# Projection pieces moved from the middle of each quarter to its end, in the attention stage of a two-layer kernel

## The chip, the cores and the metric

The kernel runs on one core of a Trainium2 chip. The metric is the device time of one execution in microseconds (us), as the median of several runs. TensorE (PE) does the matmuls, VectorE (DVE), ScalarE (ACT) and GpSimd (POOL) the rest; the sync engine's queue (SP) issues the transfers.

## The reference

Two layers on x of 8 sequences of 512 rows with 256 columns. What matters here is the attention in both, 16 heads of 16 dimensions each:

```python
def _L0_attn_ref(x, Wq, bq, Wk, bk, Wv, bv, Wo, bo, head_mask):   # layer one
    q = (x @ Wq.T + bq).reshape(b, s, HEADS, HEAD_DIM)            # k, v alike
    attn = jax.nn.softmax(jnp.einsum('bqhd,bkhd->bhqk', q, k) / 4, axis=-1)
    out = jnp.einsum('bhqk,bkhd->bqhd', attn * head_mask, v).reshape(b, s, HIDDEN)
    return out @ Wo.T + bo
def _attention(x, wq, wk, wv, wo):                                # layer two
    q = q * cos + _rotate_half(q) * sin                           # k alike
    scores = jnp.where(causal, -jnp.inf, jnp.einsum('bhqd,bhkd->bhqk', q, k) * scale)
    out = jnp.einsum('bhqk,bhkd->bhqd', jax.nn.softmax(scores, axis=-1), v)
    return out @ wo
x = _layernorm(x + attention_one(x))
h = x + _attention(_rmsnorm(x, g1), ...)
x = _layernorm(x + h + moe(_rmsnorm(h, g2)))
```

(shortened: the last line stands for the residual, the mixture of 8 experts with the two best taken per row, and the final norm.)

## The kernel before

One program runs through setup, attention of both layers, router, experts and final norm. The change is in `attention_layers` alone.

There are 16 **units** `u`: units 0 to 7 are the sequences in layer one (`plain`, unmasked), 8 to 15 the same in layer two (`causal`, masked). A unit has four **groups** `n = 4u + g` of four heads, a group four **quarters**. Every engine runs `for n in range(FIRST, LAST): for quarter in range(4)` with n from -10 to 74, so that work of several units goes on at once. In one quarter of group n TensorE does:

- **scores** of group n (`score`, L772): q and k of 49 rows, that is half the height of the array (rows 0 or 64 up), 512 columns or fewer into one of three banks `ps_s`. ScalarE takes the exponential of each into `probs` (L969), and a score waits until the exponential of the score three before is done (`free_score`).
- **maxima** for group n + 3 (`maximum`, `causal_maximum`, L777): the same product turned, at the other half of the height, into one of three banks `ps_m`; VectorE reduces each to its row maxima (L1038), and `free_maximum` is the wait alike. The row maxima shift the scores three groups later.
- the **product with v** (`weigh`, L865): `probs` times v into `ps_o`, full height, four tiles of 32 columns, 512 moving columns unmasked, in a masked unit 512, 384, 256 and 128 for the tiles 0 to 3 of k. Quarters 2 and 3 do tiles 0 and 1 of group n, quarters 0 and 1 tiles 2 and 3 of group n - 1. ScalarE moves `ps_o` out in quarter 2 (`empty_o`, L976).
- one **piece** (`a_piece`): a part of other units' work, all into the one bank `ps_x`, by the table `piece_at(n, i)`. Long pieces are `qk` (six matmuls of 512 columns, L660), `v` (L671) and `out` (L704), twelve of 256 columns; short ones are `rows` (four transposes of the maxima, L692), and in masked units `turn` (x, L681), `parts` (L713) and `logits` (L723). A piece waits until the piece before it has been moved out of `ps_x` (`piece_out`), by ScalarE (L896, L899, L907, L915, L920, L926) or VectorE (L1099, L1106, L1112, L1123, L1128), each in its `empty_piece`.

An unmasked quarter has 4 scores and 4 maxima of 512 columns. In a masked unit `score_items` lists 4, 4, 2 and 2 scores, one in each quarter being a **diagonal** bank of four blocks of 128 columns, and a quarter has 3 maxima, one of them diagonal too. `diagonals` does both: a matmul of the mask into either bank (L834, L839), then eight blocks of 128 columns that add to it, scores and maxima in turn.

Before, the order within a quarter is pairs 0 and 1, piece, diagonals, pairs 2 and 3, product with v. ScalarE empties the piece of a quarter in the same quarter: behind its last exponential in unmasked units, behind the second or the first in masked ones (`early`); VectorE in the same way behind the first or the last reduction.

Besides, ScalarE does `whiten` and `part_high` in groups g = 1 and 2 and `square` in g = 3; VectorE does `part_low` and `statistics` in g = 3, `scale_hidden` in g = 1, in masked units the two halves of the rotation (`rope_cos` in even groups, `rope_sum` in odd ones), and `invert` in quarter 1 of odd groups. GpSimd splits q and k into a high and a low half (L529, L534), normalises the result (`normalise`, L542 to L548), splits weights for later (L605, L607) and, masked, computes `part_low` (L598).

The sync queue is in order too. In even groups it issues `swap` (q32 to q_swap, L362), which waits until the last qk piece of a half is emptied, then `load_qk` (six loads into qkx, L382, which wait for the store of the same half), then x or the residual's rows, the store of o, weights, and `load_o`; in odd groups `load_rows`, stores of the inverse and of o, `load_inv`, weights and `store_qk` (L367). TensorE waits for qkx at the first maximum of each even `ahead = n + 3`, so in odd groups n. The table of pieces is

```python
(0, 0): ("turn", u + 2, 0), (0, 1): ("turn", u + 2, 1), (0, 2): ("v", u + 1, 0), (0, 3): ("v", u + 1, 1),
(1, 0): ("parts", u - 3, 1), (1, 1): ("rows", u, 1), (1, 2): ("qk", u + 2, 0), (1, 3): ("qk", u + 2, 1),
(2, 0): ("logits", u - 3, 0), (2, 2): ("out", u - 1, 0), (2, 3): ("out", u - 1, 1),
(3, 0): ("parts", u - 2, 0), (3, 1): ("rows", u + 1, 0), (3, 2): ("qk", u + 2, 2), (3, 3): ("qk", u + 2, 3)
```

Of the kernel before, what the change touches and what calls it, by code (L numbers as in the profile page):

```python
# [22 lines left out]
G, HG = 4, 4  # L23
# [185 lines left out]
def attention_layers(nc, t, xT_dram, x_dram, x1_dram, matrices):  # L209
# [16 lines left out]
    causal = lambda u: B <= u < NU  # L226
# [8 lines left out]
    def piece_at(n, i):  # L235
# [4 lines left out]
            (1, 0): ("parts", u - 3, 1), (1, 1): ("rows", u, 1), (1, 2): ("qk", u + 2, 0), (1, 3): ("qk", u + 2, 1),  # L240
            (2, 0): ("logits", u - 3, 0), (2, 2): ("out", u - 1, 0), (2, 3): ("out", u - 1, 1),
            (3, 0): ("parts", u - 2, 0), (3, 1): ("rows", u + 1, 0), (3, 2): ("qk", u + 2, 2),
# [14 lines left out]
    def emptied_piece(engine, *piece):  # L257

        engine.wait_ge(piece_out, numbers[piece] + 1)

# [4 lines left out]
    with ExitStack() as ctx:  # L265
# [373 lines left out]
        def _(pe):  # L639
# [168 lines left out]
            def causal_maximum(n, quarter, i):  # L808
# [6 lines left out]
                if i == 0:  # L815
# [7 lines left out]
            def diagonals(n, ahead, quarter):  # L823
# [4 lines left out]
                if score_here:  # L828
                    i = 2 if quarter < 2 else 1
                    kind, o, k = score_items(n // G, quarter)[i]  # L830
                    number = items(n) + scores_before(n // G, quarter) + i
# [3 lines left out]
                if maximum_here:  # L835
                    number = items(ahead) + 3 * quarter + 1
# [32 lines left out]
            for n in range(FIRST, LAST):  # L869
                for quarter in range(4):  # L870
                    for i in range(2):
                        score(n, quarter, i)
                        maximum(n + 3, quarter, i)
                        if i == 0:
# [12 lines left out]

        @block.scalar
        def _(act):
# [124 lines left out]
            for n in range(FIRST, LAST):  # L1014
                u, g = n // G, n % G
                for quarter in range(4):
                    early = (1 if quarter < 2 else 0) if causal(u) else 3
                    for i in range(4):
# [4 lines left out]
                        if i == early:  # L1023
                            empty_piece(n, quarter)
# [10 lines left out]
        def _(vector):  # L1035
# [17 lines left out]
            def causal_row_max(n, quarter, i):  # L1053
# [5 lines left out]
                if i == 0:  # L1059
# [3 lines left out]
                elif i == 1:  # L1063
# [96 lines left out]
            def empty_piece(n, quarter):  # L1160
# [686 lines left out]
```

## Time and profile before

| | |
|---|---|
| median of 3 runs | 1531.02 us (1530.84 to 1533.89) |
| profiled execution | 1533.58 us, its span 1531.9 us |
| TensorE matmuls busy | 1288.0 us, 84% of the span |
| VectorE, ScalarE, GpSimd busy | 969.1, 830.7, 685.3 us |
| mean granted TensorE clock | 0.932 of full speed |
| attention stage | to about 890 us from the start of the span |

Times in the rows are us from the start of the span unless marked ns. A row of the timeline has the start, the duration, the engine, the line of the kernel, and in brackets how long the engine was idle before and what ended that; rows of one line close together are merged, with their count behind the x. A matmul's duration includes its way through the array, so the distance between starts tells what it occupies.

### The profile page before, as it was taken

How to read it: one execution, taken by the hardware profiler on the slowest of the kernel's cores; microseconds unless marked ns; L12 is line 12 of the kernel's file. 1: busy time of each engine (PE TensorE's matmuls, PEld its weight loads, DVE VectorE, ACT ScalarE, POOL GpSimd, SP SyncE). 2: the span in 40 equal slices, each digit the busy share in tenths (PEclk: the TensorE clock that was granted, in tenths of full speed). 3: DMA queues.
4: the chain of work that ended last, by engine and by line, in shares of the span. 5: the costliest groups of instructions: out<-in, count | busy, mean ns of one | idle time of the engine just before them, and what ended most of it. 6: DMA issues, size and time to landing. Idle time of an engine off the chain costs nothing. (4 is left out here: it accounts for less than half of the span.)

```text
span 1531.9 us, 32817 instructions
## 1 busy us (share of the span) xinstructions
PE 1288.0 (84%) x11210; PEld 715.7 (47%) x11278; DVE 969.1 (63%) x1778; ACT 830.7 (54%) x1669; POOL 685.3 (45%) x713
## 2 busy tenths in 40 slices
PE   1899999999999999999999831499999999999910
PEld 0222232323233444444444310388888888888810
DVE  6478888988897788787777317343444434444346
ACT  3158788888878676666666620133443334433313
POOL 1324365546455756666564442423343343433312
PEclk9979999999999999999999965599999999999965
DMA  4426566766676878778665438191111111111136
GB/s 122 83 56 168 158 164 180 194 164 177 190 208 172 207 210 213 200 193 213 205 177 164 144 126 244 52 329 55 45 47 42 41 44 45 47 42 41 39 120 220
DMA packets 162441, 212.20 MB, mean 139 GB/s; under 512 B 28577, under 2 KB 124321, under 8 KB 162337
## 3 DMA queue, kind: packets, MB, share of 16 engines
q1 hardware_dynamic: 154848, 190.38, 45.4%
q0 software_dynamic: 7488, 20.46, 4.5%
q8 instruction: 62, 1.02, 0.3%
q14 instruction: 43, 0.34, 0.1%
HBM read 119.55 MB, written 82.58 MB: 132 GB/s over the span
## 5 line engine op out<-in xcount | busy, mean ns | idle before, releaser
L969 ACT ACTIVATE a_probs<-a_ps_s 128x512 f32<-128x512 f32 (+2 forms) x896 | 460.6, 570 | 175.6 <-PE a_ps_s L772 172.8
L1038 DVE TENSOR_REDUCE a_shift_max<-a_ps_m 128x1 f16<-128x512 f32 x512 | 320.6, 683 | 68.9 <-PE a_ps_m L777 67.5
L1555 PE MATMUL e_ps_gu<-e_xT,w_up 128*128 128x256 f16 x2574 | 298.9, 274 | 2.2 <-ACT e_xT L1610 2.1
L777 PE MATMUL a_ps_m<-a_qkx 48*128 48x128 f16 (+3 forms) x1408 | 284.0, 301 | 13.7 <-DVE a_shift_max L1038 7.7
L772 PE MATMUL a_ps_s<-a_qkx 49*128 49x128 f16 (+3 forms) x1408 | 275.6, 296 | 15.9 <-ACT a_probs L969 14.8
L1555 PEld LDWEIGHTS e_ps_gu<-e_xT,w_up 128*128 x2574 | 249.8, 98 | 36.4 <-issue 7.1
L865 PE MATMUL a_ps_o<-a_probs,a_v_one 128*32 128x512 f32 (+3 forms) x2048 | 235.5, 533 | 2.6 <-ACT a_o L976 2.5
L772 PEld LDWEIGHTS a_ps_s<-a_qkx 49*128 49x128 f16 x1408 | 90.4, 95 | 290.9 <-ACT a_probs L969 154.1
L1517 POOL DMA_INDIRECT y<-e_y,e_put x78 | 76.9, 986 | 263.3 <-DVE e_y L1644 251.4
L1577 PE MATMUL e_ps_y<-w_down,e_h 128*128 x1404 | 162.6, 273 | 8.0 <-issue 6.1
L1655 DVE TENSOR_TENSOR e_h<-e_gate,e_ps_gu 128x512 f32<-128x512 f32 (+2 forms) x156 | 82.7, 551 | 127.9 <-ACT e_gate L1618 114.3
L1618 ACT ACTIVATE e_gate<-e_ps_gu 128x512 f32<-128x512 f32 x78 | 46.6, 597 | 203.9 <-PE e_ps_gu L1555 193.9
L1577 PEld LDWEIGHTS e_ps_y<-w_down,e_h 128*128 128x128 f16 x1404 | 127.9, 97 | 40.4 <-issue 14.6
L542 POOL TENSOR_TENSOR a_o_half<-a_o_half,a_inv_half 128x512 f32<-128x512 f32 x32 | 40.7, 1271 | 236.9 <-DMA a_inv_half<-a_inv_dram 236.9
L1661 DVE TENSOR_TENSOR e_h<-e_h 128x512 f16<-128x512 f32 (+2 forms) x156 | 83.3, 555 | 98.0 <-ACT e_h L1622 43.2
L1038 DVE TENSOR_REDUCE a_neg_off<-a_ps_m 128x1 f32<-128x384 f32 (+2 forms) x256 | 138.4, 544 | 9.6 <-PE a_ps_m L777 8.7
L1038 DVE TENSOR_REDUCE a_neg_max<-a_ps_m 128x4 f32<-128x512 f32 x128 | 88.0, 687 | 51.4 <-PE a_ps_m L777 48.6
L660 PE MATMUL a_ps_x<-a_xT,w_proj 128*128 128x512 f16 x384 | 102.9, 408 | 18.6 <-POOL a_xT L510 16.1
L777 PEld LDWEIGHTS a_ps_m<-a_qkx 48*128 48x128 f16 x1408 | 84.3, 94 | 54.6 <-DVE a_shift_max L1038 36.2
L529 POOL CAST a_qk<-a_q 128x1024 f16<-128x1024 f32 x32 | 33.2, 1037 | 163.5 <-DVE a_q L1093 101.3
L1504 POOL DMA_INDIRECT e_x<-part,e_take x78 | 83.3, 1068 | 43.5 <-issue 43.2
L704 PE MATMUL a_ps_x<-w_proj,a_aT 128*128 128x256 f16 x384 | 53.2, 294 | 32.5 <-POOL a_aT L548 24.0
(191 smaller groups left out, 1583.0 us busy)
## 6 DMA issues: line engine op xcount, KB each, us to landing
a_qkx<-a_qk_dram SPq DMA_DIRECT2D x192, 128.0 KB, 4.4
a_qk_dram<-a_qk SPq DMA_DIRECT2D x32, 512.0 KB, 5.6
a_o_dram<-a_o SPq DMA_DIRECT2D x64, 256.0 KB, 3.7
a_o_half<-a_o_dram SPq DMA_DIRECT2D x32, 256.0 KB
a_inv_half<-a_inv_dram SPq DMA_DIRECT2D x32, 256.0 KB
part<-a_part SPq DMA_DIRECT2D x16, 512.0 KB, 5.8
a_q_swap<-a_q SPq DMA_DIRECT2D x64, 128.0 KB
c_rows<-y SPq DMA_DIRECT2D x16, 512.0 KB, 5.5
```

The source lines that it names most:

```text
L660: mm = pe.matmul(ps_x[:], t.w_proj[:, 4 * layer + w, wh, k, m * P:(m + 1) * P], xT[:, u % 2, xh, k, :], start=n == 0, stop=n == 5)
L772: return pe.matmul(out, kx[first:first + 49, r, pair, kt * P:(kt + 1) * P], qx[first:first + 49, r, pair, q0:q1], start=start, stop=stop)
L777: return pe.matmul(out, qx[first:first + 48, r, pair, q * P:(q + 1) * P], kx[first:first + 48, r, pair, k0:k1], start=start, stop=stop)
L865: mm = pe.matmul(ps_o[32 * j:32 * (j + 1), S - w:S], v_one[:, u % 2, kt, g * HG + j, :], probs[:, kt // 2, j, first:first + w], start=kt = ...
L969: act.activation(dst, src, ACT.Exp).then_inc(exp_out, 1)
L1038: vector.tensor_reduce(out, src, AX.X, ALU.max, negate=True).then_inc(max_out, 1)
L1504: pool.indirect_dma_start(x[:, s, half], None, t.part_dram, bass.IndirectOffsetOnAxis(ap=take[:, s, half:half + 1], axis=0)).then_inc(gath ...
L1517: pool.indirect_dma_start(t.y_dram, bass.IndirectOffsetOnAxis(ap=put[:, s, half:half + 1], axis=0), y[:, s, half], None).then_inc(stored[s ...
L1555: mm = pe.matmul(ps_gu[:, bank, kind, f % 2], w[:, ds(e, 1)].rearrange("p o f -> p (o f)"), xT[:, s, xh, k, :], start=n == 0, stop=n == 5)
L1577: mm = pe.matmul(ps_y[:, s, half], h[:, s, hh, f, half * P:(half + 1) * P], w[:, ds(e, 1)].rearrange("p o f -> p (o f)"), start=c == 0, st ...
L1655: op = vector.tensor_tensor(h32[0:rows, bank, m], gate[0:rows, bank, m], ps_gu[0:rows, bank, 1, m], ALU.mult)
L1661: op = vector.tensor_tensor(h[0:rows, s, 1, f], h32[0:rows, bank, m], h[0:rows, s, 0, f], ALU.subtract)
```

## The change

In each quarter TensorE does the diagonals first, then all pairs with the masked maxima behind pairs 1 and 2, the product with v, and last the piece. The diagonal is the first item of `score_items` in each quarter and the first of the three masked maxima. Both engines empty the piece of a quarter in the following quarter, behind its second exponential or reduction (`quarter_before`); VectorE now asks `piece_at` which piece that is. In the table, `rows` and `parts` exchange places.

```diff
-            (1, 0): ("parts", u - 3, 1), (1, 1): ("rows", u, 1), (1, 2): ("qk", u + 2, 0), (1, 3): ("qk", u + 2, 1),
+            (1, 0): ("rows", u, 1), (1, 1): ("parts", u - 3, 1), (1, 2): ("qk", u + 2, 0), (1, 3): ("qk", u + 2, 1),
-            (3, 0): ("parts", u - 2, 0), (3, 1): ("rows", u + 1, 0), (3, 2): ("qk", u + 2, 2),
+            (3, 0): ("rows", u + 1, 0), (3, 1): ("parts", u - 2, 0), (3, 2): ("qk", u + 2, 2),
+    def quarter_before(n, i):
+        return (n, i - 1) if i > 0 else (n - 1, 3)
...
-            return ((("first", 0, 0), ("first", 1, 0), ("diagonal", 1, 0), ("first", 2, 0)),
-                    (("first", 3, 0), ("second", 0, 1), ("diagonal", 0, 0), ("second", 1, 1)),
-                    (("third", 1, 2), ("diagonal", 0, 1)), (("third", 0, 2), ("diagonal", 1, 1)))[quarter]
+            return ((("diagonal", 1, 0), ("first", 0, 0), ("first", 1, 0), ("first", 2, 0)),
+                    (("diagonal", 0, 0), ("first", 3, 0), ("second", 0, 1), ("second", 1, 1)),
+                    (("diagonal", 0, 1), ("third", 1, 2)), (("diagonal", 1, 1), ("third", 0, 2)))[quarter]
... causal_maximum, diagonals, causal_row_max: item 0 is the diagonal, item 1 what was item 0
             for n in range(FIRST, LAST):
                 for quarter in range(4):
-                    for i in range(2):
+                    diagonals(n, n + 3, quarter)
+                    for i in range(4):
                         score(n, quarter, i)
                         maximum(n + 3, quarter, i)
-                        if i == 0:
-                            causal_maximum(n + 3, quarter, 0)
-                    a_piece(n, quarter)
-                    diagonals(n, n + 3, quarter)
-                    for i in range(2, 4):
-                        score(n, quarter, i)
-                        maximum(n + 3, quarter, i)
-                        if i == 3:
-                            causal_maximum(n + 3, quarter, 2)
+                        if i in (1, 2):
+                            causal_maximum(n + 3, quarter, i)
                     if quarter < 2:
                         weigh(n - 1, 2 + quarter)
                     else:
                         weigh(n, quarter - 2)
+                    a_piece(n, quarter)
... ScalarE
-                    early = (1 if quarter < 2 else 0) if causal(u) else 3
-                        if i == early:
-                            empty_piece(n, quarter)
+                        if i == 1:
+                            empty_piece(*quarter_before(n, quarter))
... VectorE
-                    early = causal((n + 3) // G)
-                        if i == (0 if early else 3):
-                            empty_piece(n, quarter)
+                        if i == 1:
+                            empty_piece(*quarter_before(n, quarter))
```

## Rows read from the trace of the kernel before

**Rows 1.** The granted clock in 40 slices of the span, in tenths.

```profile
PEclk9979999999999999999999965599999999999965
```

**Rows 2.** Busy time by stretch: window, length, engines (instructions), clock, DMA share, GB/s.

```profile
326.19:339.10 12.91, 12.32 (x82) 3.16 (x80) 12.62 (x25) 10.24 (x21) 0.00 (x0) 1.00 0.41 126
301.33:351.93 50.60, 47.51 (x341) 14.49 (x339) 44.65 (x81) 42.77 (x85) 27.65 (x28) 1.00 0.69 185
643.79:655.65 11.86, 11.75 (x138) 6.20 (x136) 9.21 (x16) 8.31 (x18) 10.46 (x9) 1.00 0.98 238
```

**Rows 3.** Timeline of TensorE in an unmasked unit.

```profile
302.32 0.39 PE L772 MATMUL a_ps_s<-a_qkx 49*128 49x512 f16 x1
...
303.40 0.39 PE L772 MATMUL a_ps_s<-a_qkx 49*128 49x512 f16 x1 [0.25 <-ACT a_probs L969]
303.60 0.39 PE L777 MATMUL a_ps_m<-a_qkx 48*128 48x512 f16 x1
303.92 1.07 PE L865 MATMUL a_ps_o<-a_probs,a_v_one 128*32 128x512 f32 x8
...
307.44 0.39 PE L772 MATMUL a_ps_s<-a_qkx 49*128 49x512 f16 x1
...
307.98 1.47 PE L660 MATMUL a_ps_x<-a_xT,w_proj 128*128 128x512 f16 x6
309.38 0.39 PE L772 MATMUL a_ps_s<-a_qkx 49*128 49x512 f16 x1
...
309.92 1.07 PE L865 MATMUL a_ps_o<-a_probs,a_v_one 128*32 128x512 f32 x8
310.92 0.39 PE L772 MATMUL a_ps_s<-a_qkx 49*128 49x512 f16 x1
```

**Rows 4.** Timeline of ScalarE and VectorE in the same stretch.

```profile
302.75 2.06 ACT L969 ACTIVATE a_probs<-a_ps_s 128x512 f32<-128x512 f32 x4
...
302.85 5.01 DVE L1038 TENSOR_REDUCE a_shift_max<-a_ps_m 128x1 f16<-128x512 f32 x8 [0.31 <-PE a_ps_m L777]
```

**Rows 5.** Groups by line on VectorE, 250 to 350.

```profile
L1155 DVE SCALAR_TENSOR_TENSOR a_part<-a_x_res,a_rms,a_part 128x256 f16<-128x256 f32 x8 | 3.8, 475 | 0.0
L1133 DVE BATCH_NORM_STATS2 a_stats<-a_x_res 128x6 f32<-128x256 f32 x8 | 3.4, 419 | 0.0
L1123 DVE TENSOR_TENSOR a_x_res<-a_ps_x,a_x_res 128x512 f32<-128x512 f32 x4 | 2.7, 681 | 0.0
```

**Rows 6.** Timeline in masked units: two stretches of TensorE, one row of ScalarE.

```profile
603.69 0.22 PE L772 MATMUL a_ps_s<-a_qkx 49*128 49x128 f16 x1
...
603.94 0.60 ACT L969 ACTIVATE a_probs<-a_ps_s 128x512 f32<-128x512 f32 x1 [0.16 <-PE a_ps_s L772]
...
644.95 0.38 PE L839 MATMUL a_ps_m<-mask_qk,ident_bf 128*128 128x512 bf16 x1
645.26 0.23 PE L772 MATMUL a_ps_s<-a_qkx 49*128 49x128 f16 x1
...
645.75 0.64 PE L865 MATMUL a_ps_o<-a_probs,a_v_one 128*32 128x256 f32 x8
646.32 0.33 PE L772 MATMUL a_ps_s<-a_qkx 49*128 49x384 f16 x1
```

**Rows 7.** Timeline of the sync queue, with TensorE's wait for a load.

```profile
598.68 2.66 SPq L382 DMA_DIRECT2D a_qkx<-a_qk_dram  x6
...
606.11 0.39 PE L777 MATMUL a_ps_m<-a_qkx 48*128 48x256 f16 x2 [0.99 <-DMA a_qkx<-a_qk_dram]
...
642.81 3.81 SPq L362 DMA_DIRECT2D a_q_swap<-a_q  x4
648.04 2.66 SPq L382 DMA_DIRECT2D a_qkx<-a_qk_dram  x6
```

**Rows 8.** Who waited for whom: us in total, times, longest; 500 to 840.

```profile
DVE a_hid L1128 <- POOL a_part L598: 17.0, 5, 4.1
...
PEld a_ps_m L777 <- DMA a_qkx<-a_qk_dram: 3.7, 4, 1.3
```

More of the change, by code:

```diff
@@ L828, in diagonals @@
                 if score_here:
-                    i = 2 if quarter < 2 else 1
-                    kind, o, k = score_items(n // G, quarter)[i]
-                    number = items(n) + scores_before(n // G, quarter) + i
+                    kind, o, k = score_items(n // G, quarter)[0]
+                    number = items(n) + scores_before(n // G, quarter)
                     s_bank = number % 3
@@ L835, in diagonals @@
                 if maximum_here:
-                    number = items(ahead) + 3 * quarter + 1
+                    number = items(ahead) + 3 * quarter
                     m_bank, m_half = number % 3, (0, 1, 1, 0)[quarter]
@@ L870, in _ @@
                 for quarter in range(4):
-                    for i in range(2):
+                    diagonals(n, n + 3, quarter)
+                    for i in range(4):
                         score(n, quarter, i)
                         maximum(n + 3, quarter, i)
-                        if i == 0:
-                            causal_maximum(n + 3, quarter, 0)
-                    a_piece(n, quarter)
-                    diagonals(n, n + 3, quarter)
-                    for i in range(2, 4):
-                        score(n, quarter, i)
-                        maximum(n + 3, quarter, i)
-                        if i == 3:
-                            causal_maximum(n + 3, quarter, 2)
+                        if i in (1, 2):
+                            causal_maximum(n + 3, quarter, i)
                     if quarter < 2:
@@ L1058, in causal_row_max @@
                 pair = 2 * (n % 2)
-                if i == 0:
+                if i == 1:
                     q = 2 - quarter // 2
@@ L1062, in causal_row_max @@
                          ps_m[:, bank, 0:2 * q * P].rearrange("p (j k) -> p j k", j=2))
-                elif i == 1:
+                elif i == 0:
                     q = 2 * (quarter // 2)
@@ L1158, in part_low, with empty_piece @@
                         op.then_inc(part_lo, 1)
-            def empty_piece(n, quarter):
-                u, g = n // G, n % G
-                if g == 0 and quarter == 1:
-                    move_x(u + 2)
-                elif g == 1 and quarter == 0:
-                    move_parts(u - 3)
-                elif g == 2 and quarter == 0:
-                    move_logits(u - 3)
-                elif g == 2 and quarter >= 2:
-                    residual(u - 1, quarter - 2)
+            def empty_piece(n, i):
+                piece = piece_at(n, i)
+                if piece is None:
+                    return
+                kind, u, k = piece
+                if kind == "turn" and k == 1:
+                    move_x(u)
+                elif kind == "parts" and k == 1:
+                    move_parts(u)
+                elif kind == "logits":
+                    move_logits(u)
+                elif kind == "out":
+                    residual(u, k)
             vector.memset(kx, 1.0).then_inc(filled, 1)
@@ L1182, in _ @@
                             causal_row_max(n + 3, quarter, i)
-                        if i == (0 if early else 3):
-                            empty_piece(n, quarter)
+                        if i == 1:
+                            empty_piece(*quarter_before(n, quarter))
                     if g == 1:
```

## The prediction, made before the changed kernel had run

> **What bounds the kernel now.** The page's slices come first: the granted clock is full through nearly all of the attention stage (the first 22 of 40) [rows 1]. The table of stretches then gives the rates: an unmasked unit of four groups takes 50.60 us, in which TensorE is busy 47.51, VectorE 44.65 and ScalarE 42.77; its group with part_low and the statistics on VectorE takes 12.91, a masked group 11.86 [rows 2]. No engine has much room, so what decides is how they interlock; that is read from the timeline.
>
> Unmasked quarters come in two kinds [rows 3]. A short one (no long piece) starts at 302.32 with pairs of a score and a maximum. Three pairs go out at once, since ps_s and ps_m have three banks each. The fourth score waits until 303.40 for the first exponential (start 302.75), the fourth maximum until 303.60 for the first reduction (start 302.85), and the product with v starts at 303.92: 1.60 after the start. Its 512 columns take 1.00 until the next quarter (below, 309.92 to 310.92). A long one starts at 307.44: two pairs, at 307.98 the piece, at 309.38 two more pairs, at 309.92 the product with v, at 310.92 the end. That is 3.48 without any wait: the 1.40 of the piece lie between the second and the third pair, and in them ScalarE and VectorE free the banks. All long pieces (qk, v, out) stand in quarters 2 and 3. In short quarters VectorE sets the pace, eight reductions back to back in 5.01 (0.626 each), ScalarE's exponentials in 0.515 [rows 4].
>
> **The change, part by part.**
>
> *A, unmasked units: four pairs without the piece among them.* The fourth maximum now waits in every long quarter, as in the short one: 1.60 until the product with v, then 1.00 and the piece's 1.40, so 4.00 for 3.48. VectorE and ScalarE then idle behind the last bank, for 2.40 of TensorE's work follows with nothing new for them. What they do besides no longer fits: the emptying of the last long piece moves into quarter 0 of the next group, which they bound already. I follow the four groups of a unit from quarter to quarter, with steps of 0.626 and 0.515, 0.6 for a move out of ps_x, 0.49 for whiten, 0.73 from a reduction's start to the fourth maximum and 0.65 from an exponential's start to the fourth score (these last two from the short quarter), 0.32 on to the product with v. Side work on VectorE is 0.68 and 0.48 and 0.42 in duration (residual, part_low, statistics) [rows 5], counted 0.60, 0.39 and 0.33, since durations overlap by some 0.09. Group 0: 2.60, 2.58, 3.98, 4.00 = 13.16. Group 1: 2.92 (the rows piece, 0.32, stands behind quarter 0), 2.61, then ScalarE is behind by the moved v, rows and two whitens, its exponential starts 1.06 into quarter 2 and that takes 4.43, last 4.00: 13.96. Group 2: 2.60, 2.88, 3.98, 4.00 = 13.46. Group 3: the residual and two rounds of part_low and statistics put VectorE's first reduction 1.17 into quarter 1 and 1.44 into quarter 2: 2.92, 3.49, 4.89, 4.00 = 15.3 against 12.91. The unit is 55.9 against 50.60, or 1.3 per group. Over 29 groups with unmasked scores and maxima that is 38, less 3 for the first three, which have few pieces and little side work, plus 6 for three groups of unmasked scores above masked maxima and for the lead-in. **A = +41.**
>
> *B, masked units: the fourth score.* Quarters 0 and 1 have four scores. Before, the fourth is free since the piece lies in between. Now the diagonal is first: the masks take 0.53 (the second starts at 644.95, the blocks 0.31 later), the last diagonal product starts at 0.71, and its exponential follows 0.25 behind the last block (603.69 to 603.94) [rows 6]. It is over at 1.56, so the fourth score starts at 1.6, where TensorE alone would reach it at 1.13: 0.45 in each of 64 quarters is 29, less 3 for the quarters without a piece, which wait now too. **B = +26.** The maxima, three a quarter, have three banks and never wait for their own quarter; VectorE (9.21 of 11.86) keeps up. Quarters 2 and 3 have two scores, and nothing waits.
>
> *C, masked units: changes of the array's shape.* From half-height products to the piece there is a gap: the long piece's six matmuls at full height fill 1.30 of 1.40, and the product with v takes 1.00 for 512 columns and 0.57 for 256 until the next start, 0.215 per 128, so 0.14 of the 0.57 is neither; about 0.1 goes into each change [rows 3, 6]. Before, a masked quarter leaves half height twice and comes back twice (piece with masks, product with v); now product with v, piece and masks stand together, and one round trip goes (0.2), while the step from the product with v (32 columns wide) to the piece is shown nowhere: 0 to 0.145. I take 0.1, as for any change of shape here, so 0.1 saved in 128 quarters. **C = -13.** The Trainium skill ("TensorE: Matmul & The Clock Gate", What happens when you issue a matmul) says that a weight load is pulled ahead of running matmuls where its row groups don't conflict or it goes into the background buffer; by that the step costs nothing, C is -26 and A is 6 less. The trace agrees for piece to mask and not for half height to full.
>
> *D, masked units: the swap.* On the sync queue the swap of q and k waits for the last qk piece, and the load of qkx for the next maxima stands right behind it. Before, that piece is emptied in quarter 3, so the swap is issued from 642.81, 3.81 long, and the load only from 648.04, since its store has to land: 1.4 of slack. Its six issues take 2.66 and TensorE goes on 4.7 us behind the last one (598.68 + 2.66 to 606.11) [rows 7]. The group began at 643.79. Now the piece is emptied behind the second exponential of the next group, at about 2.4 after its start; swap 3.8, load 2.7, landing 4.7: 13.7 after the start. An even group will be 12.3 or 12.0 long (quarter 0: 1.85 + 0.57 and a piece of 0.46 or 0.6; quarter 1: 1.92 + 0.36 and 0.46 or none; quarters 2 and 3: 1.14, then 1.00 or 0.78, then 1.31), so the first masked maximum of each odd group, and all behind it on TensorE, waits 1.6. From group 32 to 56 that is 13 times, 21, less some 4 of such waits that are there already [rows 8]. **D = +17.** What else stands behind the load (x_res, o, den) shifts with it by 2.2, and the invert, normalise and inv loads follow; the odd group starts 1.6 later, so they meet it nearly as before. Where no swap is due (unmasked q and k), GpSimd's split waits some 2 us longer, covered by its idle time (busy 27.65 of 50.60) [rows 2].
>
> *E, masked units: the residual.* VectorE stands in front of the first out piece's residual for part_low of GpSimd, 17.0 in five waits, once 4.1 (628.21), with the maxima queued behind it [rows 8]. The residual now comes in the next quarter, some 3.3 later; Of these 17, TensorE lost some 13 (VectorE catches up about 0.8 each time, an estimate), which mostly goes. **E = -13.** The waits for aT go too, included. The new places of rows and parts (quarters 0 and 1 exchanged) cost nothing: rows is ready when max_joined is, at the end of the group before, and is emptied no later; parts have a group of slack.
>
> Sum: 41 + 26 - 13 + 17 - 13 = +58, on the profiled execution's own 1533.6: 1591.6. The median of the runs is 2.6 lower, so I forecast **1589**. Router, experts and the final norm (from about 890) are untouched.
>
> **The rivals.**
> 1. *The swap is covered* (no D, or B smaller because the groups stretch past 13.7 and the load is ready): the sum falls by 17, to 1572. For it: one late even group suffices. Against: the two lengths above.
> 2. *Full-height work runs on without a gap*: C = -26, A = 35, so 1570. For it the skill's rule and piece to mask; against it, half to full.
> 3. *The clock falls.* TensorE waits more; between attention and experts, with idle stretches, the slices show 6 and 5 tenths [rows 1]. Were the mean granted clock of the some 800 us of units 0.95 where it is near 1.00, that is 5% of them, +40: 1631. Against: the waits of 0.3 to 0.8 in today's short quarters leave it full [rows 2, 3]. The same page warns, in its part on PSUM queue cycling, that small pauses between groups of matmuls make the clock swing; 50.60 us of just such pauses stand here at 1.00, so the trace doesn't bear it out.
> 4. *Faster: the gaps at changes of shape pay for all.* In about 190 quarters with a piece one round trip goes. The place is TensorE between piece and diagonal, the price 0.1 to 0.2 each, 19 to 38. It decides only from (41 + 6 + 26 + 17 - 13) / 190 = 0.4 a quarter; then some 1515 if it were 0.5. The rows show 0.1 per change.
> 5. *No change*: the waits found are taken over by slack; nothing in the 3.48 quarters shows slack on TensorE.
>
> **How the numbers follow.** Forecast 0.56 (1576 to 1606); rival 1: 0.15; rival 2: 0.13; rival 3: 0.06; rival 4: 0.06; rival 5: 0.04. Both 1 and 2 together give 1553, side work 1.5 times as heavy in A gives about 1605: the range is 1550 to 1614. A measurement here tells 0.2% from nothing. Faster 0.06, same 0.03, slower 0.91.
>
> **What would show it.** A: long unmasked quarters of about 4.0 between products with v, PEld or PE waits for a_shift_max rising, units of 56, part_low groups above 15. B: waits for a_probs of some 0.45 behind the diagonals of quarters 0 and 1. C: start of the product with v to the piece 0.1 above its own columns, or not. D: waits for DMA a_qkx of 1 to 2 in every odd masked group, the swap issued 2.4 after a group's start. E: the row of a_hid waiting for a_part small. It is wrong if ScalarE and VectorE free a bank sooner than 1.3 after a quarter's start, or if the groups' order lets the side work fall into the 2.4 of quarters 2 and 3.

## The result and the profile after

The changed kernel takes **1616.4 us** as the median of 4 runs (1613.17 to 1623.29), the kernel before 1531.2 in the same session: 1.056 times as long (95% interval 1.053 to 1.058), or 85 us more. The forecast was 1589, its range 1550 to 1614. The direction was right and the size was 27 us too small, 2 us beyond the range. The profiled execution took 1613.17 us, its span 1611.5. In the sessions below one run of diag_first (2177 us) and two of the kernel before (4257 and 3148 us) lay far from all others and are in no median or ratio.

First the page's totals and the granted clock in its 40 slices.

```profile
PE 1291.8 (80%) x11210; PEld 731.5 (45%) x11278; DVE 969.2 (60%) x1778; ACT 815.5 (51%) x1669; POOL 694.8 (43%) x713
...
PEclk9789999999999999999999995579999999999965
```

TensorE does the same work, 1291.8 us for 1288.0, in a longer span; and the slices of the attention stage are as full as in [rows 1]. A 9 leaves room, though: by the trace's own record of the clock, TensorE was at the lower of its two levels (1.2 of 2.4 GHz) in short stretches that sum, over the two halves of the stage cut below, to 31.0 us before and 20.5 us after. So the lost time is in waits, not in the clock, which settles rival 3.

Next, the stage in two halves, cut where TensorE issues the first product with v of group 0 and of group 32, and the last one. The columns are those of [rows 2]. First the kernel before, then the one after.

```profile
90.44:496.53 406.09, 385.08 (x2725) 119.80 (x2729) 353.52 (x622) 337.36 (x657) 206.83 (x193) 0.99 0.64 168
496.53:885.95 389.42, 361.94 (x3775) 164.46 (x3840) 284.38 (x508) 256.88 (x558) 227.62 (x189) 0.97 0.71 193
```

```profile
87.99:533.16 445.17, 397.50 (x2734) 133.10 (x2736) 354.25 (x624) 331.48 (x658) 207.04 (x194) 0.99 0.59 154
533.16:965.83 432.67, 362.99 (x3772) 167.72 (x3831) 282.37 (x503) 248.18 (x557) 225.69 (x189) 0.98 0.65 172
```

The unmasked half is 39.1 longer, the masked half 43.3, the lead-in 2.4 shorter, and what follows is the same. These cuts return for every experiment below. The prediction had 41 for the first (A, with the lead-in) and 17 for the second (B to E): the first half came out, the second did not.

The column PEclk, the third from the end, matters too: the masked half had 24.0 us at the lower level before (0.97) and 13.7 after (0.98), and further down the same masked order takes 389.42 us with 24.0 of them and 384.10 with 11.5. From these two I estimate 0.4 us of time for each us at the lower level, so masked halves of two executions can be 5 us apart or more for that alone.

**Unmasked.** The same view for the unit that answers to [rows 2], then for its groups 0 to 3.

```profile
300.50:356.20 55.70, 49.44 (x337) 16.10 (x336) 45.33 (x81) 42.18 (x86) 27.55 (x27) 1.00 0.62 164
...
300.50:314.20 13.70, 12.34 (x83) 4.03 (x82) 12.01 (x23) 9.92 (x21) 11.74 (x16) 1.00 0.89 221
314.20:327.90 13.70, 12.07 (x87) 4.02 (x86) 10.03 (x18) 11.27 (x24) 5.21 (x3) 1.00 0.47 151
327.90:341.20 13.30, 12.00 (x83) 3.83 (x82) 9.94 (x17) 11.38 (x25) 10.61 (x9) 1.00 0.84 195
341.20:356.20 15.00, 13.03 (x87) 4.22 (x86) 13.36 (x26) 9.61 (x21) 0.00 (x0) 1.00 0.32 97
```

55.70 for a predicted 55.9, and 13.70, 13.70, 13.30 and 15.00 for 13.16, 13.96, 13.46 and 15.3. The timeline of TensorE in a long quarter, beside that of [rows 3]:

```profile
338.30 1.48 PE L708 MATMUL a_ps_x<-w_proj,a_aT 128*128 128x256 f16 x12
339.72 0.39 PE L776 MATMUL a_ps_s<-a_qkx 49*128 49x512 f16 x1
...
340.79 0.39 PE L776 MATMUL a_ps_s<-a_qkx 49*128 49x512 f16 x1 [0.25 <-ACT a_probs L967]
...
341.24 1.07 PE L868 MATMUL a_ps_o<-a_probs,a_v_one 128*32 128x512 f32 x8
342.24 1.48 PE L708 MATMUL a_ps_x<-w_proj,a_aT 128*128 128x256 f16 x12
343.65 0.39 PE L776 MATMUL a_ps_s<-a_qkx 49*128 49x512 f16 x1
```

From 339.72 to 343.65 it is 3.93, where the prediction had 4.00 and the kernel before 3.48. The fourth score waits for the first exponential and starts at +1.07 (before, in a short quarter, +1.08), the product with v at +1.52, 0.08 sooner than predicted, since here the fourth maximum has no wait of its own. Then 2.41 follow, v and the piece, in which no bank of scores or maxima fills. VectorE meanwhile stands idle for 0.93 before the next quarter's first reduction:

```profile
344.18 1.29 DVE L1035 TENSOR_REDUCE a_shift_max<-a_ps_m 128x1 f16<-128x512 f32 x2 [0.93 <-PE a_ps_m L781]
```

**Masked.** A masked group is now

```profile
698.70:713.20 14.50, 12.23 (x132) 5.91 (x133) 8.79 (x16) 8.24 (x19) 11.69 (x10) 1.00 0.85 191
```

for 11.86 in [rows 2] and a predicted 12.0 to 12.3, before the waits of D. Who waited for whom on TensorE, 533 to 966 (us in total, times, longest):

```profile
PE a_ps_o L868 <- ACT a_o L974: 33.2, 32, 1.4
...
PE a_ps_x L664 <- ACT a_q L894: 4.7, 12, 0.4
...
PE a_ps_x L708 <- DVE a_hid L1125: 4.1, 6, 0.7
PE a_ps_x L685 <- ACT a_xT L918: 2.8, 5, 0.6
PE a_ps_x L675 <- ACT a_v_one L905: 2.8, 7, 0.4
...
PEld a_ps_m L842 <- DMA a_qkx<-a_qk_dram: 0.4, 1, 0.4
```

Before, the product with v waited, from 496 to 886, 2.5 us, and VectorE for `part_low` 27.2:

```profile
DVE a_hid L1128 <- POOL a_part L598: 27.2, 6, 10.3
...
PE a_ps_o L865 <- ACT a_o L976: 2.5, 4, 1.0
```

The product with v waits once in every masked group for `ps_o` to be moved out: 32 times, 33.2 us, and no term of the prediction has it. Behind it stand the pieces, long ones above all, which wait for `ps_x` to be emptied: 18.5 us in all such rows of TensorE, 6.7 before. The wait for the load, which term D had rise by 17 us, is 0.4. The wait for `part_low` (E) does not occur in this kernel. One instance, on TensorE and on ScalarE:

```profile
707.09 0.62 PE L685 MATMUL a_ps_x<-ident,a_x_parts 128*128 128x128 f16 x8 [0.55 <-ACT a_xT L918]
707.55 0.38 PE L837 MATMUL a_ps_s<-mask_kq,ident_bf 128*128 128x512 bf16 x1
...
708.43 0.32 PE L781 MATMUL a_ps_m<-a_qkx 48*128 48x384 f16 x1
709.74 1.06 PE L868 MATMUL a_ps_o<-a_probs,a_v_one 128*32 128x512 f32 x8 [0.99 <-ACT a_o L974]
710.74 1.48 PE L675 MATMUL a_ps_x<-w_proj,a_xT 128*128 128x256 f16 x12
```

```profile
708.51 0.60 ACT L967 ACTIVATE a_probs<-a_ps_s 128x512 f32<-128x512 f32 x1 [0.49 <-PE a_ps_s L776]
709.00 0.59 ACT L974 ACTIVATE a_o<-a_ps_o 128x512 f32<-128x512 f32 x1
```

Quarter 2 has two scores; TensorE is through with them 1.2 after its masks (707.55). The move of `ps_o` stands behind the first exponential, and that is the diagonal's: it starts 0.96 after the masks, the move ends at 709.59, and TensorE stood still for 0.99. Before, the piece of 1.4 lay in between. The first row shows the second kind of wait, here at the end of quarter 1: the piece comes before ScalarE has moved the previous one out of `ps_x`, since that move now stands behind the second exponential of this quarter (and this one, of 1024 columns, takes 1.03). The same befalls the pieces behind quarters of two scores; the qk piece at 699.94 waits 0.39.

### The profile page after: what moved, and what is told of

The parts are those of the page before. It is cut to its first block and busy times, and to the rows that moved or that the text cites. A ratio compares the mean times of both kernels' runs of the same rounds, so it can differ in the third digit from the quotient of the medians.

```text
span 1611.5 us, 32817 instructions
## 1 busy us (share of the span) xinstructions
PE 1291.8 (80%) x11210; PEld 731.5 (45%) x11278; DVE 969.2 (60%) x1778; ACT 815.5 (51%) x1669; POOL 694.8 (43%) x713
## 5 line engine op out<-in xcount | busy, mean ns | idle before, releaser
L967 ACT ACTIVATE a_probs<-a_ps_s 128x512 f32<-128x512 f32 (+1 forms) x896 | 456.2, 572 | 300.7 <-PE a_ps_s L776 299.4
L776 PE MATMUL a_ps_s<-a_qkx 49*128 49x128 f16 (+3 forms) x1408 | 263.4, 293 | 45.0 <-ACT a_probs L967 35.7
L781 PE MATMUL a_ps_m<-a_qkx 48*128 48x128 f16 (+3 forms) x1408 | 271.7, 298 | 21.4 <-DVE a_shift_max L1035 14.1
L776 PEld LDWEIGHTS a_ps_s<-a_qkx 49*128 49x128 f16 x1408 | 94.1, 94 | 244.7 <-ACT a_probs L967 149.7
L1035 DVE TENSOR_REDUCE a_neg_off<-a_ps_m 128x1 f32<-128x384 f32 (+2 forms) x256 | 131.9, 547 | 0.0
L533 POOL CAST a_qk<-a_q 128x1024 f16<-128x1024 f32 x32 | 33.2, 1038 | 210.2 <-DVE a_q L1090 147.5
L781 PEld LDWEIGHTS a_ps_m<-a_qkx 48*128 48x128 f16 x1408 | 92.0, 94 | 61.6 <-DVE a_shift_max L1035 42.0
L664 PE MATMUL a_ps_x<-a_xT,w_proj 128*128 128x512 f16 x384 | 97.7, 392 | 23.1 <-POOL a_xT L514 15.9
L1503 POOL DMA_INDIRECT e_x<-part,e_take x78 | 92.2, 1182 | 43.6 <-issue 43.6
L868 PEld LDWEIGHTS a_ps_o<-a_probs,a_v_one 128*32 128x32 f32 x2048 | 42.1, 108 | 92.5 <-ACT a_probs L967 64.7
```

The lines of the kernel that those rows point to most:

```text
L664: mm = pe.matmul(ps_x[:], t.w_proj[:, 4 * layer + w, wh, k, m * P:(m + 1) * P], xT[:, u % 2, xh, k, :], start=n == 0, stop=n == 5)
L776: return pe.matmul(out, kx[first:first + 49, r, pair, kt * P:(kt + 1) * P], qx[first:first + 49, r, pair, q0:q1], start=start, stop=stop)
L781: return pe.matmul(out, qx[first:first + 48, r, pair, q * P:(q + 1) * P], kx[first:first + 48, r, pair, k0:k1], start=start, stop=stop)
L868: mm = pe.matmul(ps_o[32 * j:32 * (j + 1), S - w:S], v_one[:, u % 2, kt, g * HG + j, :], probs[:, kt // 2, j, first:first + w], start=kt = ...
L967: act.activation(dst, src, ACT.Exp).then_inc(exp_out, 1)
L1035: vector.tensor_reduce(out, src, AX.X, ALU.max, negate=True).then_inc(max_out, 1)
```

## The experiments

Diffs are against the changed kernel, except where the kernel before is named. "Before" is its median in the same session. A masked half is read from one profiled execution, a median from 4 to 12 runs.

**The two halves apart.** A predicate `late(n)` chooses, group by group, the new order (diagonals first, piece last, emptied a quarter later, new places in the table) or the old one.

```diff
# shortened: the old items, emptying and table for the old groups are left out
+    late = lambda n: n < 32          # h_unmasked;   n >= 32 in h_masked
...
-                    diagonals(n, n + 3, quarter)
+                    if late(n): diagonals(n, n + 3, quarter)
...
+                        elif i == 1: a_piece(n, quarter); diagonals(n, n + 3, quarter)
...
-                    a_piece(n, quarter)
+                    if late(n): a_piece(n, quarter)
```

> The new order (with its emptying and its table of pieces) only in groups before 32, where the scores are unmasked; from group 32 on the order of the kernel before. Theory (each stretch loses by its own waits, in unmasked quarters the fourth pair's): about 35 us above the kernel before, 1566, with long quarters of 3.93 and the unit at 55.7. Rival (the emptying one quarter later sets back the chain of transfers from q and k to the next unit, so the loss of one stretch comes from the other's delay as well): well below or above, 1550 or less, or over 1580.

> The reverse: the order of the kernel before until group 31, the new one from group 32 on. Theory: about 43 us above the kernel before, 1574, and the two losses add to what the whole change costs (78 to 85). Rival: the sum of the two is clearly smaller or larger than the whole.

New order in layer one alone: 1572.6 (ratio 1.027, 1.024 to 1.031), +41. New order in layer two alone: 1576.5 (1.030, 1.027 to 1.034), +45. Together 86 for the whole change's 85: the halves add up, the first costs what A said, the second more than twice what B to E said. The windows of h_masked show where:

```profile
90.28:497.53 407.25, 384.95 (x2734) 120.03 (x2739) 354.85 (x625) 337.66 (x658) 207.08 (x193) 0.99 0.64 168
497.53:930.11 432.58, 362.37 (x3772) 167.02 (x3831) 285.00 (x507) 247.70 (x556) 226.67 (x189) 0.98 0.65 173
```

**The sync queue (D).** In `load_first` the load of qkx is issued ahead of the swap.

```diff
-                    swap((n + 6) // 2)
                     load_qk((n + 4) // 2)
+                    swap((n + 6) // 2)
```

> The changed kernel with the load of qkx ahead of the swap in the sync queue. The predicted term D (swap late, load behind it, TensorE waits 1.6 in each of 13 odd masked groups): about 17 to 20 us less than the changed kernel, 1597. What the trace of the changed kernel suggests instead (swap issues take 2.5, not 3.8, and no wait for qkx is seen): no difference within 3 us.

1617.3 (1.057, 1.054 to 1.060), as the changed kernel; the masked half 432.35 for 432.67. D is refuted. The queue in the changed kernel shows why, for a group whose masks stood at 701.25:

```profile
703.70 2.48 SPq L366 DMA_DIRECT2D a_q_swap<-a_q  x4
706.28 2.87 SPq L386 DMA_DIRECT2D a_qkx<-a_qk_dram  x6
```

The swap is issued 2.45 after the group's start, as predicted (2.4), but takes 2.48 for the 3.81 of [rows 7]; the issues of the load end at 709.15 and the last of its data land at 714.2, 12.95 after the start, and the group is over 14 long. The 3.81 was no odd row: between 520 and 800 the kernel before takes 2.8 to 4.8 for each of its 12 swaps, the changed kernel 2.5 for each of 10. So the issue got shorter with the change; what in the queue's surroundings does that was not tested. Rival 1 had named the other part: the groups stretch past the load.

**The piece ahead of the product with v.** `piece_before_v` only exchanges the last two steps of a quarter.

```diff
+                    a_piece(n, quarter)
                     if quarter < 2:
                         weigh(n - 1, 2 + quarter)
                     else:
                         weigh(n, quarter - 2)
-                    a_piece(n, quarter)
```

> The changed kernel with the piece ahead of the product with v instead of behind it, still behind all four pairs. Theory (the four pairs without the piece among them cost the fourth pair's wait, wherever the piece then stands): unmasked units stay at 55 us or more; in masked quarter 2 the wait for empty_o (26.5 in all) is covered by the piece, but the piece itself comes sooner and waits longer for the one before to be emptied, about 0.5 in each quarter 3: in all 1600 to 1625. Rival (it is the distance of the piece from the pairs, product with v and piece in one run of 2.4 us, that starves ScalarE and VectorE; split, each gap is short): at least 25 less than the changed kernel.

1688.6 (1.104, 1.101 to 1.108), 72 slower than the changed kernel. The expectation (1600 to 1625) missed. It had named both effects, the piece covering the wait for `ps_o` and the piece waiting longer for its own bank, but the second only with 0.5 in each quarter 3 of masked groups. Its timeline in an unmasked unit, and rows of its table of waits over the whole run:

```profile
371.70 1.47 PE L664 MATMUL a_ps_x<-a_xT,w_proj 128*128 128x512 f16 x6 [0.55 <-ACT a_q L897]
```

```profile
PE a_ps_x L664 <- ACT a_q L894: 16.2, 16, 1.2
...
PE a_ps_x L675 <- ACT a_v_one L905: 12.6, 16, 1.2
...
PE a_ps_x L675 <- DVE a_xT L1096: 10.4, 8, 1.5
```

The piece arrives 1.0 sooner, by the product with v, and its bank is not empty. Over the whole run TensorE waits 133.7 us for `ps_x` to be emptied, 44.2 in the changed kernel, and 5.5 for `ps_o` instead of 34.9: 60 more together, most of the 72. So the product with v is what lets a piece stand behind a quarter whose emptying comes in the next: there is one bank `ps_x`, and every place for a piece has a price in how far it is from its emptying.

**The two waits of the masked quarters.** `o_first` empties `ps_o` ahead of the first exponential of quarter 2; `piece_first` empties the piece of the quarter before behind the first exponential or reduction instead of the second; `both_first` does both. All in masked groups alone.

```diff
+                        if quarter == 2 and i == 0 and causal(u):          # o_first
+                            empty_o(n - 1)
...
-                        if quarter == 2 and i == 0:
+                        if quarter == 2 and i == 0 and not causal(u):
...
-                        if i == 1:                                         # piece_first, ScalarE
+                        if i == (0 if causal(u) else 1):
                             empty_piece(*quarter_before(n, quarter))
...
-                        if i == 1:                                         # piece_first, VectorE
+                        if i == (0 if causal(n // G) else 1):
```

> The changed kernel with ScalarE moving ps_o out ahead of the first exponential of quarter 2 in masked groups, not behind it. Theory (in masked quarter 2 the set of two scores is over in 1.1 us and the product with v then waits for ps_o to be emptied, 26.5 us in 26 waits; the piece had covered this before): 20 to 27 us less than the changed kernel, about 1592. Rival (the masked loss is the fourth score alone, and the wait for ps_o only takes over time that would be lost anyway): within 5 us of it.

> The changed kernel with the piece of the quarter before emptied behind the first exponential or reduction in masked groups, nothing else. Theory: 8 to 16 us less than the changed kernel, 1600 to 1608, so that this and the run with ps_o alone add up to the run with both. Rival: nothing gained.

> The same, and in masked groups the piece of the quarter before is emptied behind the first exponential or reduction instead of the second. Theory (the piece at the end of a quarter of two scores arrives before the one before it has left ps_x, 0.4 in each quarter 3 and 0.5 in quarters 1 with a wide move): another 8 to 16 us less than the run with ps_o alone, about 1580. Rival: the earlier move delays the second exponential and with it the fourth score, and nothing is gained.

| | median | ratio to before (95%) | masked half | of it at the lower clock | TensorE's waits for ps_o, ps_x |
|---|---|---|---|---|---|
| kernel before | 1531.2 | 1 | 389.42 | 24.0 | 2.5, 6.7 |
| changed kernel | 1616.4 | 1.056 (1.053 to 1.058) | 432.67 | 13.7 | 33.2, 18.5 |
| o_first | 1600.2 | 1.046 (1.043 to 1.049) | 413.06 | 10.2 | 5.8, 26.3 |
| piece_first | 1599.2 | 1.045 (1.041 to 1.048) | 418.20 | 20.4 | 32.6, 3.4 |
| both_first | 1577.8 | 1.032 (1.029 to 1.035) | 392.34 | 3.4 | 8.1, 5.9 |

The moves take 19.6 and 14.5 us out of the masked half, together 40.3 of the 43.3 that the change had added; by the medians of the whole kernel it is 16, 17 and 39. The waits fall by 19.6, 15.7 and 37.7. With the wait for `ps_o` gone, some of it comes back at `ps_x` (26.3 for 18.5), but the two moves are additive to within 3 us of waits; the larger excess in the halves goes with the time at the lower clock. By the medians o_first gains less than the 20 to 27 expected, and both_first more than the 8 to 16 expected on top of it (22). In both_first the half is

```profile
536.32:928.66 392.34, 363.24 (x3834) 167.25 (x3831) 277.81 (x503) 244.72 (x557) 226.90 (x189) 1.00 0.71 190
```

against 389.42 before, with 20 us less at the lower clock, so by the estimate of 0.4 for each the order itself may still cost up to 11 us. Its timeline of TensorE shows what is left, B:

```profile
702.63 0.38 PE L837 MATMUL a_ps_s<-mask_kq,ident_bf 128*128 128x512 bf16 x1
...
704.24 0.33 PE L776 MATMUL a_ps_s<-a_qkx 49*128 49x384 f16 x1
704.50 0.64 PE L868 MATMUL a_ps_o<-a_probs,a_v_one 128*32 128x256 f32 x8
704.96 0.39 PE L696 MATMUL a_ps_x<-ident,a_shift_max 128*8 128x128 f16 x4
```

The fourth score starts 1.61 after the masks (predicted 1.6, and 1.13 if it were free). Of the 63 such quarters found in this trace 52 have 1.61 or about 1.74.

**B and C against each other.** `diag_mid` is both_first with the diagonals back behind pair 1 (piece still last): the first exponential comes early again, and the array changes between half and full height twice a quarter again.

```diff
-                    diagonals(n, n + 3, quarter)
                     for i in range(4):
                         score(n, quarter, i)
                         maximum(n + 3, quarter, i)
-                        if i in (1, 2):
-                            causal_maximum(n + 3, quarter, i)
+                        if i == 0:
+                            causal_maximum(n + 3, quarter, 0)
+                        elif i == 1:
+                            diagonals(n, n + 3, quarter)
+                        elif i == 3:
+                            causal_maximum(n + 3, quarter, 2)
```

> The run with both moves first, with the diagonals (scores and maxima) back behind pair 1 as in the kernel before; the piece stays last. Terms B and C of the prediction by themselves: the fourth score of masked quarters 0 and 1 then waits for the first one's exponential, over long before (26 us less), and one change of shape more per quarter comes back (13 to 26 more), so between 13 less and no difference, 1565 to 1578. Rival (the fourth score's wait of 0.45 was covered by ScalarE being late anyway): 10 us or more above it.

```profile
534.65:913.92 379.27, 366.02 (x3838) 159.83 (x3840) 284.25 (x505) 249.17 (x557) 227.38 (x189) 1.00 0.73 198
```

1560.3 (1.019, 1.015 to 1.023), 5 below the expected range of 1565 to 1578. The masked half is 379.27: 13.1 less than in both_first, both with 3.4 us at the lower clock; the medians of the whole kernel are 17.5 apart. It is also 10.2 less than before the change, but that half had 24.0 us at the lower clock: by the estimate above some 8 of the 10 go with the clock.

**The parts one by one, the piece left in the middle.** `diag_first` only does the diagonals first (piece between pairs 1 and 2, emptied in its own quarter, the old table). `piece_third` has the piece between pairs 2 and 3; in masked groups its pieces are emptied later too, by VectorE behind the last reduction and by ScalarE, in quarters 0 and 1, behind the last exponential (diag_first: behind the second).

```diff
                         if i in (1, 2):
                             causal_maximum(n + 3, quarter, i)
+                        if i == 1:                       # diag_first;   i == 2 in piece_third
+                            a_piece(n, quarter)
...
-                    a_piece(n, quarter)
...
-                            empty_piece(*quarter_before(n, quarter))
+                            empty_piece(n, quarter)
# shortened: the old table, and the i at which each engine empties the piece, as told above
```

> Diagonals first alone: the piece stays between pairs 1 and 2, is emptied in its own quarter (behind the last exponential unmasked, the second masked) and the table of pieces is the one before. Theory (all loss comes from what the piece no longer covers, the order of the diagonals costs nothing by itself): within 8 us of the kernel before, 1523 to 1540. Rival (diagonals first by themselves make the fourth score wait): 15 us or more above it.

> Diagonals first and the piece behind pair 2 (and the last masked maximum), ahead of the fourth score, emptied in its own quarter behind the last exponential or reduction. Theory: the piece still lies before the fourth pair and covers its wait, three pairs fit into three banks, so 1520 to 1545; where the last exponential now waits for the piece in masked quarters 2 and 3 some us may be lost. Rival (any piece later than the middle starves the two engines): 1560 or more.

diag_first 1535.4 (1.0045, 1.003 to 1.007), its halves 407.61 and 391.36, so +1.5 and +1.9, though with 6.8 us at the lower clock in the masked half. Diagonals first cost 0.45%, 6 to 7 us, while the piece stands in the middle; so most of B's 26 is a wait that the piece had covered. piece_third 1543.2 (1.010, 1.007 to 1.013), with halves that part:

```profile
88.47:491.08 402.61, 385.89 (x2738) 129.85 (x2737) 354.38 (x625) 338.51 (x659) 207.60 (x193) 0.99 0.64 171
491.08:891.29 400.21, 377.43 (x3830) 165.01 (x3831) 282.32 (x503) 253.29 (x556) 226.72 (x189) 0.96 0.69 187
```

The unmasked half is 3.5 shorter than before, the masked one 10.8 longer (31.8 us of it at the lower clock, and the emptying later as well: which of these it is was not separated).

**What that suggests.** `third_unmasked` is the kernel before with the piece between pairs 2 and 3 in layer one, nothing else.

```diff
-                    a_piece(n, quarter)
+                    if n >= 32:
+                        a_piece(n, quarter)
                     diagonals(n, n + 3, quarter)
...
+                        if i == 2 and n < 32:
+                            a_piece(n, quarter)
```

> The kernel before with the piece behind pair 2 instead of pair 1 in unmasked groups (until group 31), nothing else; masked groups as before. Theory (in unmasked quarters only the fourth pair needs cover, and a stretch of three pairs, piece, one pair and product with v leaves one wait fewer than two and two; the run with the piece third in all groups had units of 49.5 for 50.6): 4 to 9 us less than the kernel before, 1522 to 1527. Rival (what its unmasked units gained was the other emptying or order of diagonals): no difference.

1525.8 (12 runs, 1519.5 to 1531.5; before 1531.1): ratio 0.9973, 0.9953 to 0.9993. It beats the kernel before by 0.3%, as expected, and the changed one by more. Its unit and its masked half, where no instruction has moved, are

```profile
286.80:336.68 49.88, 47.36 (x338) 15.64 (x336) 44.73 (x81) 42.94 (x85) 27.50 (x27) 1.00 0.69 183
...
492.85:876.95 384.10, 360.22 (x3838) 161.75 (x3840) 280.12 (x508) 256.81 (x557) 228.20 (x189) 0.99 0.72 196
```

for 50.60 [rows 2] and 389.42; the unmasked half is 402.56, 3.5 shorter than before, as in piece_third. Three pairs go out at once, as many as there are banks, and the piece stands where the fourth would wait. The two together, this order in layer one and that of diag_mid in layer two, were not run; diag_mid's own saving there lies between 2 and 10 us, depending on what the clock is given.

**The residual alone (E).** `resid_late` is the kernel before, with VectorE taking the masked out pieces behind its last reduction of the quarter, not the first.

```diff
-                        if i == (0 if early else 3):
+                        out_here = early and n % G == 2 and quarter >= 2
+                        if i == (2 if out_here else 0 if early else 3):
                             empty_piece(n, quarter)
```

> The kernel before, with VectorE taking the out pieces of masked units behind its last reduction of the quarter instead of the first. Theory for term E (the residual waits for GpSimd's part_low, 17.0 us in five waits, with the maxima queued behind it; later by some 1.5 us each, it lets three more reductions pass): 4 to 10 us less than the kernel before, 1522 to 1527. Rival (the wait of VectorE was covered, or the piece behind out 0 waits instead): no difference.

1539.2 (1.004, 1.001 to 1.007): slower by 0.4% where 4 to 10 us less were expected. The wait of `a_hid` for `a_part` fell from 27.2 to 13.6, and nothing came of it. TensorE waits for the bank as before (L704, 5.9 then) and now also ahead of the next piece (L713, a row that the kernel before does not have); these 2.2 us explain a part of the loss, the rest is open.

```profile
DVE a_hid L1128 <- POOL a_part L598: 13.6, 4, 10.6
...
PE a_ps_x L704 <- DVE a_hid L1128: 5.8, 5, 2.0
...
PE a_ps_x L713 <- DVE a_hid L1128: 2.2, 5, 0.4
```

## Why the prediction was right and wrong

**A, right.** +36.7 for the lead-in and the unmasked half, 41 when made alone, against 41. Each part of its mechanism is in the rows: the wait for the first exponential, 3.93 for 4.00 in a long quarter, late reductions behind v and the piece, 15.0 for 15.3 in the group with part_low. Group 0 is longer than worked out (13.70 for 13.16) and the others a little shorter, so part of the agreement of the sum is errors that cancel.

**B, right in size as far as it goes.** 1.61 for 1.60 in the quarter shown, 1.61 or 1.74 in most of the others. The step that failed is its last sentence, "Quarters 2 and 3 have two scores, and nothing waits". I went through banks of scores and maxima there, and not through the other two, `ps_o` and `ps_x`, that this change brings closer to their emptying. A quarter with two scores gives ScalarE no time: TensorE is at the product with v 1.2 after the masks, the first exponential starts at 0.96, and the move of `ps_o` behind it ends 2.04 after them. That is the missing term, 19.6 us by o_first, and the second one is the piece that finds `ps_x` not yet emptied, 14.5 by piece_first. Together they are 40.3 us by the halves and 39 by the medians. They are why the forecast is too small; D's 17, which did not come, hid part of it: the error of 27 is the difference of two larger ones, and that it is no larger is luck.

**C, consistent, not measured by itself.** diag_mid against both_first takes B away and puts one round trip of shapes in: predicted 26 - 13 = 13, measured 13.1 by the halves and 17.5 by the medians. That both are of that size rests on B's 0.48 in 64 quarters; the difference alone is shown. From the product with v to the piece the starts are 1.00 apart for 512 columns (341.24 to 342.24), as they were to half height [rows 3], and 0.46 to `rows` for 256 columns (704.50 to 704.96), where to half height it was 0.57 [rows 6]. By the 0.215 per 128 columns of the prediction that leaves 0.14 beside the columns in front of a long piece and 0.03 in front of `rows`. The rows are typical: over the stage of the changed kernel 1.00 is the median before each kind of long piece (22 to 44 times), and in both_first 0.57 that for 256 columns before the short `turn` and `logits`, 0.46 that before `rows` (15 times). So the step I had put at 0.1 is as dear as the step to half height, but for one kind of piece; why `rows` differs is open. The rule that I weighed there (the Trainium skill, "TensorE: Matmul & The Clock Gate", What happens when you issue a matmul), a weight load pulled ahead of running matmuls, would have made both free. The trace agrees in front of `rows` and not in front of a long piece.

**D, wrong, and its rival 1 right.** Three of its four numbers held (issued at 2.45 for 2.4, load 2.9 for 2.7, landing 5.05 for 4.7); the swap was 1.3 shorter than before the change, and groups of over 14 us for 12.3 left room. The failed step is the fixed 3.8 for an issue that the change itself moves. load_first shows that nothing of the 85 is there.

**E, the wait went; its worth is not shown.** The 27.2 us of that wait are gone in the changed kernel, but in the faster both_first and diag_mid 8.6 and 12.6 of them are back, so the slower stage is part of the reason. both_first differs from before by B + C + E, predicted 0, measured +2.9, or some 11 at equal time at the lower clock; diag_mid by E and the order of piece and v, predicted -13, measured -10.2, or some -2 at equal clock (both are estimates). resid_late shows that taking the emptying late is not enough by itself. What of the 10.2 is E, what the place of piece and product with v, and what the clock isn't separated.

**Rivals 3, 4 and 5** fell: the time at the lower clock did not grow, TensorE's busy time is as before, and no slack took the waits. Two slips in the prediction's sums change nothing: D's terms add up to 13.6, not 13.7, and rival 3's 40 is added to 1591.6 where the forecast was 1589.

The masked half by parts: B + C + E 2.9, and 40.3 for the two waits. That they add up to the 43.3 is no test, since both are differences to both_first; the test is in TensorE's waits for `ps_o` and `ps_x`: 51.7 in the changed kernel, 9.2 before, so 42.5 more. With 39.1 and -2.4 the halves make 80, as do the spans (1611.5 and 1531.9).

## What to carry to other kernels

When a block of work moves behind another, list every buffer whose emptying it used to cover, not only those of the loop that it leaves: here the scores' banks gave A and B, but the banks `ps_o` and `ps_x`, not looked at, cost as much again. Look at the shortest iteration first, since there the same order has the least cover. In the unmasked units here the best place for filler work was behind as many producers as there are banks (the piece behind three pairs, with three banks); in the masked ones that was not shown. The emptying of a single bank belonged early in the consumer's queue: one item earlier, in two places, gave back 39 of 85 us. And an issue time, like a wait, belongs to the place in the queue where it was read.

## What the runs showed of the hardware

Four issues of the same transfer took 2.5 us in every masked group of the changed kernel (703.70 is one) and 2.8 to 4.8 in those of the kernel before, between 520 and 800, where they stand elsewhere against the other transfers ([rows 7]); the six of the load took 2.7 to 2.9 there before and 2.9 to 3.4 after. The cause of the difference was not tested.

Waits of 0.25 to 1.0 in each quarter of TensorE, in a stage 80 us longer, left the granted clock at 1.00 in the stretches shown, and its mean at 0.935 for 0.932. There are short stretches at the lower level in every one of these kernels, and how many differs between executions: in the masked half 24.0 us in the kernel before and 11.5 with the same order in third_unmasked, 389.42 and 384.10 us long; 3.4 in both_first. Compare the clock column before a difference of a few us is put down to an order.
